# Reciprocals and reciprocal roots of the attention stage taken from ScalarE's logarithm and exponential

## The reference

```python
h = relu(layernorm(x))                    # (x - mean) / sqrt(var + 1e-5)
q, k, v = h @ Wq + bq, h @ Wk + bk, h @ Wv + bv
alpha = sum_c(q[dst] * k[src]) / sqrt(32) # one score per edge and head
ea = exp(alpha - segment_max(alpha, dst)[dst])
alpha = ea / (segment_sum(ea, dst)[dst] + 1e-16)
x = x + segment_sum(v[src] * alpha, dst) + h @ Wskip + bskip
```

## Time and profile before

| | before |
|---|---|
| time, median of 3 runs | 1663.34 us (1662.32 to 1664.62) |
| the profiled execution's own time | 1664.58 us |
| its span in the profile | 1662.8 us |
| busy share of the span: TensorE, VectorE, ScalarE, GpSimd | 88%, 81%, 61%, 65% |
| mean granted TensorE clock | 0.975 of full speed |

### The profile page before, as it was taken

How to read it: one execution, slowest core, us unless ns; L and a number is a source line. 1 busy time by engine, 2 the same in 40 slices (tenths; PEclk the granted TensorE clock), 3 DMA queues, 4 the chain that set the end, 5 groups by cost and what they waited for, 6 DMA issues and landing times. The chain is left out here.

```text
span 1662.8 us, 34477 instructions
## 1 busy us (share of the span) xinstructions
PE 1470.4 (88%) x10545; PEld 1263.5 (76%) x10546; DVE 1347.6 (81%) x3688; ACT 1016.5 (61%) x2501; POOL 1083.1 (65%) x1202
## 2 busy tenths in 40 slices
PE   5888898699999999999999974899998999998996
PEld 4666777688888888888888863777776777777775
DVE  8879665299999999999999994677776777777675
ACT  5777888556555565656665513566665666665663
POOL 2554442577777777777777605777777777777772
PEclk9999999899999999999999996999999999999999
DMA  8899887556666666666666516677666767667672
GB/s 219 274 274 313 284 300 262 157 160 180 189 174 192 175 188 183 178 182 182 182 174 185 156 45 148 148 160 174 162 163 150 171 160 172 161 158 170 149 164 68
DMA packets 162552, 302.85 MB, mean 182 GB/s; under 512 B 104113, under 2 KB 107703, under 8 KB 157524
## 3 DMA queue, kind: packets, MB, share of 16 engines
q1 hardware_dynamic: 121503, 201.19, 41.9%
q0 software_dynamic: 40896, 99.90, 24.9%
HBM read 196.84 MB, written 104.12 MB: 181 GB/s over the span
## 5 line engine op out<-in xcount | busy, mean ns | idle before, releaser
L803 POOL DMA_INDIRECT sb_kv<-kv_rows,sb_src_all x500 | 492.9, 986 | 187.1 <-issue 131.3
L831 POOL DMA_INDIRECT sb_kv<-x_rows,sb_src_all x500 | 473.8, 948 | 209.3 <-issue 109.1
L1710 ACT ACTIVATE sb_hn<-sb_xn 100x128 f32<-100x128 f32 x500 | 240.5, 481 | 265.9 <-DMA sb_kv<-x_rows,sb_src_all 225.1
L1713 ACT ACTIVATE sb_vw<-sb_kv 128x128 f32<-128x128 f32 x500 | 239.6, 479 | 0.0
L1638 ACT ACTIVATE sb_hn<-sb_xn,sb_nstat 100x128 f32<-100x128 f32 x500 | 231.5, 495 | 0.0
L1400 DVE COPY sb_hT<-ps_b 128x400 f32<-128x400 f32 x250 | 142.2, 569 | 96.1 <-PE ps_b L2005 95.3
L1797 PE MATMUL ps_b<-sb_w,sb_memberT 128*125 128x256 f32 x800 | 201.6, 391 | 18.3 <-DVE sb_xn L921 9.2
L1660 ACT COPY sb_memberT<-ps_b 100x512 f32<-100x512 f32 x150 | 75.8, 506 | 205.7 <-PE ps_b L1885 205.7
L1797 PEld LDWEIGHTS ps_b<-sb_w,sb_memberT 128*125 128x125 f32 x800 | 146.2, 193 | 41.7 <-issue 14.7
L2005 PE MATMUL ps_b<-sb_member,sb_vw 128*128 128x100 f32 x1000 | 173.8, 278 | 0.0
L2005 PEld LDWEIGHTS ps_b<-sb_member,sb_vw 128*128 128x128 f32 x1000 | 157.4, 198 | 9.8 <-issue 9.8
(11 more groups left out here) (184 smaller groups left out, 3103.0 us busy)
## 6 DMA issues: line engine op xcount, KB each, us to landing
kv_rows<-sb_kv SPq DMA_DIRECT2D x26, 1120.0 KB
sb_xn<-x_rows SPq DMA_DIRECT2D x50, 507.8 KB
sb_xn<-in_x SPq DMA_DIRECT2D x50, 500.0 KB
out_rows<-sb_xo SPq DMA_DIRECT2D x49, 500.0 KB
x_rows<-sb_xo SPq DMA_DIRECT2D x24, 1015.6 KB
sb_kv<-in_edge_attr SPq DMA_DIRECT2D x500, 32.0 KB
sb_kv<-in_x SPq DMA_DIRECT2D x28, 560.0 KB
kv_rows<-sb_xn SPq DMA_DIRECT2D x13, 1120.0 KB
```

The costliest lines, as they stand in the source:

```text
L803: pool.indirect_dma_start(out=kvs[:, k % 4, t, :], out_offset=None, in_=kv_rows, in_offset=bass.IndirectOffsetOnAxis(ap=src_all[:, n:n + 1 ...
L831: pool.indirect_dma_start(out=xs1[:, k % 4, t, :], out_offset=None, in_=x1, in_offset=bass.IndirectOffsetOnAxis(ap=src_all[:, n:n + 1], ax ...
L1710: nc.scalar.activation(hn1[:, t, :], xn1[:, k % 4, t, 0:D], ACT.Relu, scale=xn1[:, k % 4, t, D:D + 1], bias=xn1[:, k % 4, t, D + 1:XW]).th ...
L1713: nc.scalar.activation(hs1[:, t, :], xs1[:, k % 4, t, 0:D], ACT.Relu, scale=xs1[:, k % 4, t, D:D + 1], bias=xs1[:, k % 4, t, D + 1:XW]).th ...
```

## The change

Of the softmax, `tot + 1e-16` and the reciprocal leave VectorE: ScalarE takes `Ln(tot + 1e-16)` and then `Exp(-1 * that)`. Of the statistics, the integer guess and two of three Newton rounds leave VectorE: ScalarE takes `Ln(var)` and `Exp(-0.5 * that)`, and one Newton round follows on VectorE. ScalarE's step runs these behind `exps`: the roots (turns only) at once, the inverse sums after two more ReLUs, and `copy_q(k + 1, 0)`, which stood right behind `exps`, now comes behind the inverse sums. TensorE's `turn_member` of groups 1 and 2 moves from behind `turn_alpha` to in front of `aggregate`, and VectorE's `members(k + 1, 1)` from behind `head_sums` to in front of `weigh`.

```diff
-STAT_STEPS (14) steps of x1 statistics, N_SOFT = 8
+X1_STEPS = 7
+N_SOFT = 6
...
+            pool.memset(tiny[:], 1e-16).then_inc(const_made, 1)
...
             def soft_step(k, n):
+                elif n == 5:
+                    dve.wait_ge(A.inverse, 2 * (k + 1))
...
-                elif n == 5:
-                    ins = dve.tensor_scalar(tot_e[:], tot[:], 1e-16, None, ALU.add)
-                elif n == 6:
-                    ins = dve.reciprocal(rtot[:], tot_e[:])
...
             def x1_stat_step(m, n):
+                if n == 3:
+                    dve.wait_ge(A.root, 2 * (m + 1))
...
+                if n < 3:
+                    ins = stat_math(n, st[0:NODES, m % 2, :, :], rstd, shift, slice(0, 2 * B), NODES)
+                elif n == 3:
+                    ins = dve.tensor_tensor(square, root[:], root[:], ALU.mult)
+                elif n == 4:
+                    ins = dve.scalar_tensor_tensor(part, square, -0.5, v, ALU.mult, ALU.mult)
+                elif n == 5:
+                    ins = dve.scalar_tensor_tensor(rstd, part, 1.5, root[:], ALU.add, ALU.mult)
+                else:
+                    ins = stat_math(STAT_STEPS - 1, None, rstd, shift, slice(0, 2 * B), NODES)
...
# VectorE step0(k): the order after the change, from scores(k, 0) on
+ scores 0 / stats 0 / scores 1 / stats 1 / soft 0 / stats 2 / soft 1 / soft 2 / members(k+1, 0) / soft 3 / soft 4
+ stats 3, 4, 5 / scores 2 / soft 5 (weights) / stats 6 / members(k+1, 1) / weigh / head_sums / finish, x1_stats
...
# ScalarE
+            def inverse_sums(k):
+                act.wait_ge(A.soft, N_SOFT * k + 5)
+                nc.scalar.activation(log_tot[:], tot[:], ACT.Ln, bias=tiny[:]).then_inc(A.inverse, 1)
+                act.wait_ge(A.inverse, 2 * k + 1)
+                nc.scalar.activation(rtot[:], log_tot[:], ACT.Exp, scale=-1.0).then_inc(A.inverse, 1)
+
+            def roots(m):
+                act.wait_ge(A.stat, X1_STEPS * m + 3)
+                nc.scalar.activation(log_var[:], var[0:NODES, :], ACT.Ln).then_inc(A.root, 1)
+                act.wait_ge(A.root, 2 * m + 1)
+                nc.scalar.activation(root[:], log_var[:], ACT.Exp, scale=-0.5).then_inc(A.root, 1)
...
                 if real(k - 1):
                     exps(k - 1)
+                if k % 2 == 1 and 0 <= (k - 3) // 2 < BATCHES // 2:
+                    roots((k - 3) // 2)
+                relus(k + 2, 1, 3)
+                if real(k - 1):
+                    inverse_sums(k - 1)
                 if nxt:
                     copy_q(k + 1, 0)
-                relus(k + 2, 1, 3)
-                if nxt:
                     copy_q(k + 1, 1)
...
# TensorE
                     skip(k - 1, 1)
+                if nxt:
+                    turn_member(k + 1, 1)
+                    turn_member(k + 1, 2)
+                if prev:
                     aggregate(k - 1, 0)
                     aggregate(k - 1, 1)
                     skip(k - 1, 2)
                     aggregate(k - 1, 2)
                 if this:
                     turn_alpha(k)
                 if nxt:
-                    turn_member(k + 1, 1)
-                    turn_member(k + 1, 2)
                     gather_q(k + 1, 0)
                     gather_q(k + 1, 1)
```

More of the change, by code:

```diff
@@ L54 @@
 ITEM = {"h0": 1, "h1": 2, "q0": 3, "q1": 4, "m0": 5, "q2": 6, "m1": 7, "m2": 8}
-N_SOFT = 8
+N_SOFT = 6
 T_DVE = (STAT_STEPS + 8 + 1 + STAT_STEPS, 5)
@@ L199, in build @@
         tot = sb("tot", [BH, WIN])
-        tot_e = sb("tot_e", [BH, WIN])
+        log_tot = sb("log_tot", [BH, WIN])
         rtot = sb("rtot", [BH, WIN])
@@ L211, in build @@
         nwt = sb("nwt", [128, 2, 2 * B])
+        log_var = sb("log_var", [NODES, 2 * B])
+        root = sb("root", [NODES, 2 * B])
         nstat = sb("nstat", [NODES, TILES, 2])
@@ L215, in build @@
         minus_half = sb("minus_half", [ROWS, 2 * B])
+        tiny = sb("tiny", [BH, 1])
         src_all = sb("src_all", [128, TILES], I32)
@@ L404, in __init__ @@
                 self.exp = s("exp_done")
+                self.root = s("reciprocal_root_step")
+                self.inverse = s("inverse_sums_step")
                 self.wT = s("weights_turned")
@@ L601, in store @@
             def store(m):
-                sp.wait_ge(A.stat, STAT_STEPS * (m + 1))
+                sp.wait_ge(A.stat, X1_STEPS * (m + 1))
                 rows = x1[2 * GROUP * m:2 * GROUP * (m + 1), :].rearrange("(s p t) c -> p s (t c)", s=2, t=B)
@@ L739, in _ @@
             pool.memset(minus_half[:], -0.5).then_inc(const_made, 1)
-            pool.wait_ge(const_made, 8)
+            pool.memset(tiny[:], 1e-16).then_inc(const_made, 1)
+            pool.wait_ge(const_made, 9)
             pool.affine_select(out=ident[:], in_=ident[:], compare_op=ALU.not_equal, fill=1.0, base=0,
@@ L932, in search_first @@
                     if n == 0:
-                        dve.wait_ge(const_made, 9)
+                        dve.wait_ge(const_made, 10)
                         dve.wait_ge(heads_spread, 1)
@@ L1262, in x1_stats @@
                 if g == 0:
-                    wait(dve, A.stat, STAT_STEPS * (m - 2) + 1)
+                    wait(dve, A.stat, X1_STEPS * (m - 2) + 1)
                     if m < 2:
@@ L1273, in x1_stat_step @@
                     dve.wait_ge(A.bn, 2 * (m + 1))
-                wait(dve, A.stat, STAT_STEPS * m + n)
+                if n == 3:
+                    dve.wait_ge(A.root, 2 * (m + 1))
+                else:
+                    wait(dve, A.stat, X1_STEPS * m + n)
                 both = xo[:, 2 * (m % 2):2 * (m % 2) + 2, :, :]
-                stat_math(n, st[0:NODES, m % 2, :, :], both[:, :, :, D].rearrange("n s t -> n (s t)"),
-                          both[:, :, :, D + 1].rearrange("n s t -> n (s t)"), slice(0, 2 * B), NODES
-                          ).then_inc(A.stat, 1)
+                rstd, shift = (both[:, :, :, D + i].rearrange("n s t -> n (s t)") for i in range(2))
+                square, part, v = nwt[0:NODES, 0, :], nwt[0:NODES, 1, :], var[0:NODES, :]
+                if n < 3:
[6 more added lines that the diff above has]
+                    ins = dve.scalar_tensor_tensor(rstd, part, 1.5, root[:], ALU.add, ALU.mult)
+                else:
+                    ins = stat_math(STAT_STEPS - 1, None, rstd, shift, slice(0, 2 * B), NODES)
+                ins.then_inc(A.stat, 1)
             def step0(k):
@@ L1300, in step0 @@
                     soft_step(k - 1, 1)
-                stats(3)
                 if prev:
                     soft_step(k - 1, 2)
-                stats(4)
                 if nxt:
                     members(k + 1, 0)
-                stats(5)
                 if prev:
                     soft_step(k - 1, 3)
-                stats(6)
                 if prev:
                     soft_step(k - 1, 4)
-                stats(7)
+                stats(3)
+                stats(4)
+                stats(5)
+                if this:
+                    scores(k, 2)
                 if prev:
                     soft_step(k - 1, 5)
[L1316 to L1325, removed]
+                stats(6)
+                if nxt:
+                    members(k + 1, 1)
                 if prev:
                     weigh(k - 1)
-                stats(12)
                 if this:
                     head_sums(k)
-                stats(13)
-                if nxt:
-                    members(k + 1, 1)
                 if prev:
@@ L1350, in last_steps @@
                 scores(k, 1)
+                stats(0)
+                stats(1)
+                stats(2)
                 for n in range(N_SOFT):
@@ L1353, in last_steps @@
                 scores(k, 2)
-                stats(0)
                 weigh(k - 1)
-                stats(1)
                 head_sums(k)
                 for n in range(N_SOFT):
-                    stats(n + 2)
+                    if n + 3 < X1_STEPS:
+                        stats(n + 3)
                     soft_step(k, n)
@@ L1364, in last_steps @@
                 finish(k - 1, 2)
[L1365 to L1368, removed]
+                for g in range(3):
+                    x1_stats(k - 1, g)
                 finish(k, 0)
@@ L1374, in last_steps @@
                 x1_stats(k, 2)
-                for n in range(STAT_STEPS):
+                for n in range(X1_STEPS):
                     x1_stat_step(m, n)
@@ L1612, in table_last_rows @@
                                banks[2 + n % 4][0:ROWS, :].rearrange("p (t c) -> p t c", t=2)).then_inc(P.kv_act, 1)
-            act.wait_ge(const_made, 9)
+            act.wait_ge(const_made, 10)
             nc.scalar.activation(er[0:1, 0:1], ones[0:1, 0:1], ACT.Exp)
@@ L1701, in _ @@
                 step0(k)
+            roots(BATCHES // 2 - 1)
             def relu1(k, t):
@@ L1820, in turn_windows @@
                 ins.then_inc(idx_turned, 1)
-            pe.wait_ge(const_made, 9)
+            pe.wait_ge(const_made, 10)
             pe.wait_ge(w0_load, 16 * 4)
```

## The result

The changed kernel takes 1980.64 us (median of 4 runs, 1976.95 to 1982.11) against 1663.98 us: a ratio of 1.1896, 95% interval 1.1869 to 1.1923. 1950 us was predicted, with a range of 1820 to 2120.

What follows compares the result with a forecast made beforehand. Between 320 and 1000 us VectorE (busy 585 of 600 us) and TensorE (566) were nearly full. Plain steps 79, turns 200 and last steps about 9 us added 288 us, giving 1950 us, range 1820 to 2120.

Steps and rivals of the forecast that it cites:

- The sum: Whole kernel: 25 plain steps x 3.15 = 79, 23 turns x 8.7 = 200, last steps about 9; 288 us added.
- A load per function, 150 in all: ScalarE: every new Ln, and every Exp behind one, has a table load before it; 150 loads, 192 us.
- Rival A: Behind each ScalarE table load: up to 1.63 us more, 245 us in all, giving 2195 us; chance 0.15.
- The chain, steps 1 to 6: From TensorE's transposes through scans, loads, q copy and third project_q to the turn of weights: plain step 16.5 us, turn 19.9.
- Step 2: VectorE, waiting for aggregates pushed back by the moved turn_member: loses 1.2 us a step, as much as it saved.
- The prices of the activations: ScalarE's new logarithms and exponentials: 0.31 us each, bounds 0.2 and 0.44, at most +-25 us over 150 instructions.
- The clock: TensorE's work after six us of idle in each turn: +2.4 us per turn; none for plain steps with 2.8 us idle.
- C: ScalarE: one set serves both functions, two loads in all; +45 us, 1709 us, copy_q still waiting behind the scans; chance 0.08.
- D: One set, inverse sums ending before TensorE wants the q copy; TensorE's 12.9 us bound the step, 1630 us; chance 0.06.
- ScalarE has room by its total: ScalarE in the stage: 7.95 us of work in a 13.3 us step; room at the new work's place left open.
- The signs: Profile after: 151 loads, ScalarE busy up about 240 us, TensorE idle 2.8 and 6 us, VectorE's share about 65%.

Runs made afterwards that it cites:

- run 5: Changed kernel, loads kept, with 10 or 26 unread matmuls per step where TensorE idles before its third project_q: 1876.86 us, ratio 1.1255 to the kernel before.
- run 1: Changed kernel plus one instruction loading a table set with both Exp and Ln ahead of the first exponential: 1689.66 us, ratio 1.0138 to the kernel before.
- run 8: Changed kernel with the logarithm of the roots replaced by an exponential, saving 50 loads, output not the reference's: 1923.09 us, ratio 1.1532 to the kernel before.
- run 6: Kernel before plus two table loads a step where ScalarE idles for the membership tiles: 1664.09 us, ratio 0.9995.
- run 7: Kernel before plus two table loads a step right behind the exponential, in front of copy_q(k+1, 0): 1719.94 us, ratio 1.0326.

## Why the prediction was right

* *The sum.* On the profiled executions 317 us were added (1664.6 to 1982.1), 288 predicted: 25 plain steps at 4.6 make 116 (79 predicted), 23 turns at 8.3 make 191 (200), and 10 are left for the two ends (9). By cause, some 104 us are the low clock (run 5), 23 stay without the loads (run 1), and the 190 between are what 150 loads last, 192 us.
* *A load per function, 150 in all.* The count is 150 and the one from the start, each 1283 ns. What the trace of before could not show, and what was taken on trust at more than 8 in 10, is settled: each of the 75 logarithms behind an Exp and each of the 75 exponentials behind an Ln has its load, while the roots' 50 activations have none where both are exponentials (run 8: 101 loads in all). So the set in place at an Exp has no Ln here, and the set picked for Ln has no Exp. Run 1 asked for one set by name and has a single load for the same 75 pairs: a set with both exists, and it was not picked here without being told.
* *Rival A, something behind each load.* Measured at nothing: two loads one behind the other take 2.57 us (run 6), and the gap behind a load is 0.01 us where no data is waited for (604.97 + 1.28 to 606.26 us there; 711.88 + 1.28 to 713.17 us, load to logarithm, in the changed kernel).
* *The chain, steps 1 to 6.* With the clock held (run 5) a plain step takes 16.01 us and a turn 19.56; 16.5 and 19.9 were worked out, 20 us too much in all. The links are those named: in the plain step shown the transposes of the normed rows start at 10.1 us and not at 7.9, since the clock is low before them, and from there on each follows as listed. Step 2 (VectorE loses by the moved membership tiles what it saved) was right as a wait, 0.8 to 1.1 us a step, but undoing the move gave 9 us and not the 1 us a step that this would make.
* *The prices of the activations.* 0.31 us was taken for all four. Measured: 0.401 for the logarithm with its bias as a column, 0.309 for the exponential behind it, 0.22 for the roots' two. In sum nearly the same.
* *The clock, the term of the sum that was mis-sized.* It was put at 2.4 us in each of the 23 turns, 55 us, and at none in plain steps with their 2.8 us of idle, for which no reason was given. The 2.4 was an estimate from the one place at hand: behind 3.89 us of idle the clock was at 0.5 until about 982.7 us, and the 5 us from 977.7 on held some 2.5 us of work. That told that 3.89 us is enough, not that less isn't. A spell costs 2.1 us (run 5), nearly as priced, but the 3.0 us of idle in a plain step bring one too: 48 spells or 102 us in all, 47 more than predicted. The chain was 20 us too long in exchange, so 1953 + 47 - 20 = 1980 for the 1982 measured. That these two errors have opposite signs is luck: with the chain as it measured, the forecast would have been 1930.
* *Rivals C and D* are kernels with one set. C, the order as given: 1709 worked out, 1690 measured. D, TensorE's own time once 0.7 us are found: with the copy early and the old order of the membership tiles 1659, with the sums earlier 1652 (1647 by its ratio), not 1630. D took 13.85 us for a turn of the kernel before; from one turn of the weights to the next it is 13.5 on the mean, so only 1638 could be hoped for. The rest is a step of 13.09 us and not 12.9: TensorE is 96% busy, and the small waits for `finish` and for the copy of the transposed rows remain.
* *ScalarE has room by its total.* It had, and two loads a step in that room cost nothing (run 6), 54 us on the chain (run 7): place, not sum, made the loss.
* *The signs.* ScalarE's busy time rose by 230 us (240 said), TensorE idled 3.0 and 6.6 us (2.8 and 6), and the wait was for the copy of q. VectorE's share fell to 60% (65 said). The plain step took 18.0 us and not 16.5, since the clock falls there too.

## What to carry to other kernels

Before a function moves to ScalarE, count how often its table set changes in the order of that engine's instructions, and name a set that holds all of them ahead of the first one: here one instruction was worth some 290 us (run 1). Work moved to an engine with much idle time was free here where that engine idled and not on the chain (two loads a step: nothing in run 6, 54 us in run 7); draw the chain from the new instruction to the next wait on it, and look at which copy stands behind it in the queue. Where a new wait makes TensorE idle some 3 us per step, as here, add the low clock behind it to the price (2 us a step in this kernel), and if the wait can't go, try matmuls that nobody reads in it: in run 5 they held the clock at 1.00 and took 104 us off.

## What was not expected of the hardware

An idle of 3.0 us between busy stretches was enough for the granted clock to fall to 0.5 for 3.4 or 6.4 us of the work that followed, at once or up to 0.9 us after the work had begun; waits of 1.0 to 1.3 us in every step (run 7) left it at 1.0. And 36 unread matmuls per pair of steps made the kernel 104 us faster (run 5). Within this stage the length of a spell, 3.4 to 6.4 us, did not follow the length of the idle in front of it (3.0, 3.9 or 6.6 us). Why spells behind equal idles differ, so that plain steps vary from 17.6 to 18.4 us, no run shows. A table load, last, began ahead of its activation's wait (at 1302.35 us for a logarithm at 1314.23), so it can hide where the data comes late, and the activation at 713.17 us followed its load after 0.01 us: nothing of the load's own stood between.
